# Score sums of batches 0 to 3 on TensorE by accumulating transposes, and two GpSimd product batches instead of three

## What is computed

```python
# s: attention over the HEADS of one token (16 x 16 scores for each token)
q = rope(xn @ Wq + bq);  k, v = split((xn @ Wdown + bdown) @ Wup + bup);  k = rope(k)
att = softmax(einsum('bthd,btgd->bthg', q, k) / sqrt(8))
s = einsum('bthg,btgd->bthd', att, v).reshape(B, T, 128) @ Wout + bout
# g: silu of a block over the other axis: attention along the batch axis, then a
# mixture of 8 experts (2 per token, 1280 rows of room each)
g = silu(h1 + moe_out)
```

## Time and profile before

| | us |
|---|---|
| median of 3 runs (404.27 to 406.10) | 405.15 |
| the profiled execution | 404.89 |
| its span, first to last instruction | 403.0 |
| VectorE busy | 367.4 |
| TensorE busy | 300.0 |
| GpSimd busy | 248.8 |
| ScalarE busy | 175.8 |

### The profile page before, as it was taken

One profiled execution on the slowest core, in us unless ns is written; L12 is line 12 of the kernel. 1 busy time (PEld: TensorE's weight loads), 2 busy tenths in 40 slices (PEclk: granted clock), 3 DMA queues, 4 the chain that ended last, 5 costly groups with the idle time before them and its releaser, 6 DMA issues.

```text
span 403.0 us, 5161 instructions
## 1 busy us (share of the span) xinstructions
PE 300.0 (74%) x1734; PEld 237.3 (59%) x1734; DVE 367.4 (91%) x499; ACT 175.8 (44%) x388; POOL 248.8 (62%) x268
## 2 busy tenths in 40 slices
PE   0846989495974473636267999999999999999890
PEld 0744567374663372236156679687779669668740
DVE  4999899979697999999999999999899999996666
ACT  2657383734172721110011667557672756561050
POOL 2397881892000577777773785587797777775271
PEclk9959899797896856959569899999999989999996
DMA  7599980000000111111113943213331321111936
GB/s 198 139 213 199 279 254 2 2 0 1 2 0 0 33 54 48 53 53 55 53 53 103 297 109 115 68 54 100 93 101 46 114 72 54 39 54 48 339 104 182
DMA packets 53719, 38.09 MB, mean 95 GB/s; under 512 B 5497, under 2 KB 50366, under 8 KB 53694
## 3 DMA queue, kind: packets, MB, share of 16 engines
q1 hardware_dynamic: 49086, 28.25, 28.0%
q0 software_dynamic: 4608, 9.51, 7.0%
HBM read 16.55 MB, written 21.20 MB: 94 GB/s over the span
## 4 chain that ended last, share of the span: by engine, by line
DVE 67%; PE 13%; issue 11%; ACT 5%; POOL 2%; DMA 2%; DVEq 0%; POOLq 0%; ACTq 0%
DVE prod L305 13%; DVE prod L297 12%; DVE score L651 12%; PE banks L831 4%; DVE stat L404 3%; DVE score L471 3%; POOL expert_rows L1420 2%; DVE score L638 2%; DVE hsum L675 2%; PE banks L992 2%; DVE hmax L669 2%; DVE prod L493 2%; PE banks L769 1%; DVE xn_all L526 1%; DVE flat L508 1%
## 5 line engine op out<-in xcount | busy, mean ns | idle before, releaser
L1392 POOL DMA_INDIRECT slot_rows<-rows_all,scatter_at x64 | 62.9, 982 | 60.5 <-DVE scatter_at L625 41.3
L1420 POOL DMA_INDIRECT expert_rows<-flat,to_at x80 | 79.8, 998 | 24.8 <-issue 20.9
L305 DVE TENSOR_TENSOR prod<-score,banks 128x2048 f32<-128x2048 f32 x32 | 70.9, 2268 | 3.5 <-PE banks L992 3.5
L992 PE MATMUL banks<-c_identf,prod 128*128 128x128 f32 x512 | 61.0, 282 | 13.2 <-DVE prod L305 13.2
L992 PEld LDWEIGHTS banks<-c_identf,prod 128*128 128x128 f32 x512 | 59.4, 147 | 14.3 <-DVE prod L305 14.3
L1355 POOL TENSOR_TENSOR prod<-rows_all,block_kv 128x64 f32<-128x64 f32 (+3 forms) x64 | 48.6, 794 | 16.1 <-ACT block_kv L1123 16.0
L297 DVE TENSOR_TENSOR prod<-banks,qkv_h 128x2048 f32<-128x2048 f32 x24 | 53.8, 2283 | 0.5
L651 DVE TENSOR_REDUCE score<-prod 128x512 f32<-128x4096 f32 x12 | 53.0, 4420 | 0.4
L962 PE MATMUL banks<-flat 128*128 128x512 f32 (+1 forms) x96 | 38.9, 550 | 4.4 <-ACT flat L1269 2.2
L856 PE MATMUL banks<-wx,qkv_h 128*128 128x128 f32 x192 | 31.8, 330 | 9.2 <-ACT qkv_h L1142 7.7
L831 PE MATMUL banks<-prod,c_identf 128*128 128x448 f32 (+7 forms) x128 | 37.8, 452 | 0.0
(11 more groups left out here) (196 smaller groups left out, 496.1 us busy)
## 6 DMA issues: line engine op xcount, KB each, us to landing
slot_rows<-prod SPq DMA_DIRECT2D x20, 264.0 KB, 7.9
flat<-slot_rows SPq DMA_DIRECT2D x16, 264.0 KB, 3.4
expert_rows<-prod SPq DMA_DIRECT2D x8, 512.0 KB, 6.0
flat<-expert_rows SPq DMA_DIRECT2D x8, 512.0 KB, 9.0
xn_all<-in_x SPq DMA_DIRECT2D x4, 512.0 KB, 4.8
flat<-in_w SPq DMA_DIRECT2D x16, 128.0 KB, 2.2
out<-rows_all SPq DMA_DIRECT2D x7, 256.0 KB, 3.2
expert_rows<-flat,to_at POOLq DMA_INDIRECT x80, 2.2
```

The lines of the kernel that those rows point to most:

```text
L305: return eng.tensor_tensor(value_pair(a // 2)[:, a % 2, :].rearrange("p (g h d) -> p g h d", g=H, h=H), p.rearrange("p h g -> p g h").unsq ...
L992: i = M.matmul(head_bank(s, p)[:, a * P:(a + 1) * P], value_pair(p)[:, a % 2, g * D:(g + 1) * D], C["identf"][:], is_transpose=True, start ...
L1392: Q.indirect_dma_start(slots_d, bass.IndirectOffsetOnAxis(ap=scatter_at[:, k, n:n + 1], axis=0), z2x[:, h, s, part], None, element_offset= ...
L1420: Q.indirect_dma_start(expert_d, bass.IndirectOffsetOnAxis(ap=to_at[:, e % 3, a:a + 1], axis=0), ye[:, e % 2, a, :], None).then_inc(ye_out ...
```

## The change

TensorE sums the score products of all pairs of batches 0 to 3. VectorE writes the products of such a pair with the channel outermost; TensorE transposes each 128 x 128 block with accumulation over the eight channels, which gives the sums turned (`turn_scores`); ScalarE copies them to SBUF (`keep_scores`); four transposes turn them back into PSUM (`turn_back`); VectorE takes maximum and difference from there. The reductions of these pairs are gone. GpSimd keeps batches 5 and 6; the second pair of batch 4 goes to VectorE. The order is rewritten on three engines: TensorE's projections of k now wait for `index_done` and stand between the new groups, and batch 2's `sum_values`, batch 1's `attention_out`, and the projections of v for batch 3 and q for batch 5 stand ahead of expert 0. Expert 0 additionally waits for `differences(3)`, since banks 0 and 1 hold scores until then.

```diff
-PE_SCORES, SCORE_BANK = 1, 0
-POOL_SCORES = {4: 0, 5: 1, 6: 3}
+PE_SCORES = (0, 1, 2, 3)
+POOL_SCORES = {5: 0, 6: 2}
...
-EXPONENTIAL_AFTER = {1: 3, 3: 4, 4: 5, 6: 6}
-COPY_AFTER = {0: 5, 2: 6}
-TURN_AT = {1: 2, 3: 3, 4: 4, 6: 5}
-OUT_AFTER = {0: 1, 2: 2, 4: 3, 5: 4, 7: 5}
-SUMS_AFTER = {1: 2, 3: 3, 4: 4, 6: 5}
-V_AFTER = {0: 3, 2: 4, 4: 5, 5: 6, 7: 7}
-Q_AFTER = {0: 5, 2: 6, 4: 7}
+EXPONENTIAL_AFTER = {1: 4, 3: 5, 4: 6, 6: 7}
+COPY_AFTER = {1: 6}
+TURN_AT = {1: 3, 3: 4, 5: 5}
+OUT_AFTER = {0: 2, 2: 3, 4: 4, 6: 5}
+SUMS_AFTER = {1: 3, 3: 4, 5: 5}
+V_AFTER = {0: 4, 2: 5, 4: 6, 6: 7}
+Q_AFTER = {1: 6, 2: 7}
...
-            return prodB if (s, p) <= (PE_SCORES, 0) else prodC
+            return pool_prod if s in PE_SCORES and p == 1 else prodC
...
+                if s in PE_SCORES:
+                    wait_past(dve, "scores_turned", 2 * (s - 1) + p + 1)
...
+            def turn_scores(s, p):
+
+                pe.wait_ge(W["q_read"], 2 * s + p + 1)
+                wait_past(pe, "row_diff", s)
+                for i in range(2):
+                    for c in range(2):
+                        at = slice((2 * i + c) * P, (2 * i + c + 1) * P)
+                        for d in range(HD):
+                            m = M.matmul(bank[p][:, at], score_pair(s, p)[:, i, (2 * d + c) * P:(2 * d + c + 1) * P], C["identf"][:],
+                                         is_transpose=True, start=(d == 0), stop=(d == HD - 1))
+                m.then_inc(W["scores_turned"], 1)
+
+            def turn_back(s, p):
+
+                pe.wait_ge(W["scores_kept"], 2 * s + p + 1)
+                for j in range(TT):
+                    i = M.transpose(bank[p][:, j * P:(j + 1) * P], turned_scores[:, p, j * P:(j + 1) * P], C["identf"][:])
                 i.then_inc(W["qk_summed"], 1)
...
+            pe.wait_ge(W["row_diff"], len(PE_SCORES))
             q_read(2)
             for e in range(E):
                 expert(e)
...
+            def keep_scores(s, p):
+                act.wait_ge(W["scores_turned"], 2 * s + p + 1)
+                A.copy(turned_scores[:, p], bank[p]).then_inc(W["scores_kept"], 1)
```

More of the change, by code:

```diff
@@ L655, in differences @@
             def differences(s):
-                if s == PE_SCORES:
+                if s in PE_SCORES:
                     half = TT * H // 2
-                    parts = [(rows(bank[SCORE_BANK]), slice(0, half)), (rows(score[:, s % 2, half * H:]), slice(half, 2 * half))]
-                    dve.wait_ge(W["qk_summed"], 1)
-                    for src, at in parts:
+                    parts = [(rows(bank[p]), slice(p * half, (p + 1) * half)) for p in range(2)]
+                    for p, (src, at) in enumerate(parts):
+                        dve.wait_ge(W["qk_summed"], 2 * s + p + 1)
                         i = V.tensor_reduce(hmax[:, s % 2, at], src, AX_X, ALU.max)
@@ L733, in _ @@
             pairs(0, 1)
+            pairs(1, 0)
+            differences(0)
+            pairs(1, 1)
             for s in range(S):
[L735 to L741, removed]
                 if s == S - 2:
-                    differences(s + 1)
+                    differences(S - 1)
                 totals(s)
@@ L748, in _ @@
                 values(s, 1)
+                if s + 1 < S - 1:
+                    differences(s + 1)
+                if s + 2 < S:
+                    pairs(s + 2, 0)
+                    pairs(s + 2, 1)
+                if s < S // 2 - 1:
+                    normalize(s)
             for p in range(2):
@@ L1038, in attention_out_last @@
                 i.then_inc(W["attn_ready"], 1)
+            pe.wait_ge(W["index_done"], 1)
+            project_k(1)
+            project_k(2)
+            turn_scores(0, 0)
+            project_k(3)
+            turn_scores(0, 1)
+            project_k(4)
+            turn_back(0, 0)
+            project_k(5)
+            turn_back(0, 1)
             project_v(1)
-            for s in range(1, S):
-                project_k(s)
+            project_k(6)
             project_q(2)
+            project_k(7)
+            turn_scores(1, 0)
             project_q(3)
-            pe.wait_ge(W["index_done"], 1)
+            turn_scores(1, 1)
             pe.wait_ge(W["k_kept"], S)
-            sum_scores()
             turn_sums(0)
+            turn_back(1, 0)
+            turn_back(1, 1)
             sum_values(0, 0)
             sum_values(0, 1)
+            turn_scores(2, 0)
+            turn_scores(2, 1)
             project_q(4)
+            turn_back(2, 0)
+            turn_back(2, 1)
             attention_out(0)
@@ L1057, in _ @@
             sum_values(1, 1)
+            turn_scores(3, 0)
+            turn_scores(3, 1)
+            project_q(5)
+            turn_back(3, 0)
+            turn_back(3, 1)
+            attention_out(1)
+            project_v(3)
+            turn_sums(2)
+            sum_values(2, 0)
+            sum_values(2, 1)
+            pe.wait_ge(W["row_diff"], len(PE_SCORES))
             q_read(2)
@@ L1308, in _ @@
             keep_k(1)
+            keep_k(2)
             rows_of_slots(2)
-            keep_k(2)
+            keep_scores(0, 0)
+            keep_k(3)
+            keep_scores(0, 1)
+            keep_k(4)
+            keep_k(5)
             rows_of_slots(3)
-            for s in range(3, S):
-                keep_k(s)
             exponentials(0)
+            keep_k(6)
+            keep_k(7)
+            keep_scores(1, 0)
+            keep_scores(1, 1)
             widen_share(0)
@@ L1322, in _ @@
             exponentials(2)
+            keep_scores(3, 0)
+            keep_scores(3, 1)
+            copy_q(5)
+            keep_attention(1)
+            widen_share(2)
+            keep_share(2)
+            exponentials(3)
             for e in range(E):
@@ L1330, in _ @@
                     copy_q(COPY_AFTER[e])
-            exponentials(7)
             for s in (S - 2, S - 1):
```

40 lines of the change are left out of this document (17 added, 23 removed).

## The result

The changed kernel takes 393.89 us in the median (390.71 to 396.68), beside 405.62 us for the kernel before: a ratio of 0.963, with a 95% interval of 0.953 to 0.973. The forecast was 394.0. The ratios leave out executions more than 1.5% above the fastest of the same kernel (the profiled one of the changed kernel is among these), so they are not the quotients of the medians.

A forecast was written before the change was run, and what follows sets the result against it. It took TensorE's expert stage as the bound: -11.43 moved work, -1.22 old waits, +0.8 and +0.7 new waits make -11.15 us, from 405.15 to 394.0 us. Forecast 390 to 398.5 (70%), wider range 390 to 403.

The forecast's parts named there:

- TensorE's stage bounds, not VectorE's sum: In the expert stage, TensorE's 139.1 us set the time; over half of VectorE's 26.5 us saving would not be seen.
- The rival with all 26.5 us in it (378.7): VectorE was the only bound, so its whole net saving of 26.5 us shows: 378.7 us; chance 4%.
- -11.43 us of moved work: Work leaving TensorE's expert stage: value sums of batch 2 6.99, output and two projections 3.84, turned sums 0.60 us.
- The waits: TensorE's two waits for VectorE go (-1.22 us); new ones come at `tail_start` (+0.8) and behind expert 0 for `normalize(2)` (+0.7).
- A term that I set to nothing: Clock at expert 0's products: a TensorE that comes warm gains up to 1.6 us, left outside the sum.
- Expert 0's start: VectorE waits 3.5 us, `values(2)` ends at 212.8, `sum_values(2)` at 219.8; expert 0 starts when its rows land, as before.
- The margin of 0.7 us: Between the end of `sum_values(2)` and expert 0's start: 0.7 us, with every further microsecond paid in full.
- Restarts of the clock: Rival: short TensorE waits in batches 0 and 1 drop the clock, four restarts cost 8 us, about 401 us; chance 15%.
- the lower level through the stage: Rival: TensorE's clock stays low through most work ahead of the experts, near 411 or up to 445 us; chance 7%.
- GpSimd sets nothing: GpSimd loses a product of 2 x 4.53 us and a wait of 8.2; its last scatters still follow expert 7.
- The tail unchanged: From `tail_start` to the end the code is the same and still takes 43 us.
- VectorE idle ahead of `values(7)`: Near the end VectorE stands idle 15 us or more in all, as `values(7)` needs the first half of `sum_values(6)`.

The follow-up runs named there:

- moves_back: Changed kernel with the five TensorE groups moved back behind expert 0, score sums still on TensorE: median 404.75 us, 1.003 of the kernel before.
- spare_later_exp: spare_stage with ScalarE's exponentials of batch 6 one expert later, behind expert 5: median 393.86 us, 257.6 us from the first score product.
- before_moves: Kernel before with only the five TensorE groups moved ahead of the experts, score sums left on VectorE: median 426.82 us, 1.046 of before.
- before_two: Kernel before with GpSimd making score products of batches 5 and 6 only, VectorE those of batch 4: median 407.94 us, 0.996 of before.
- six_first: Changed kernel with the turning and value sums of batch 6 ahead of the tail's start products: median 392.51 us, 255.9 us from the first score product.
- pool_three: Changed kernel with GpSimd making score products of batches 4, 5 and 6 as before: median 408.39 us, 272.0 us from the first score product.
- spare_early: Changed kernel with one unused 4.42 us VectorE reduction added behind batch 1's value products, ahead of the experts: median 400.68 us.
- spare_stage: Changed kernel with one unused 4.42 us VectorE reduction added behind batch 4's value products, in mid expert stage: median 395.01 us.
- after_again: Changed kernel measured a second time with no edit: median 392.77 us, 0.968 of the kernel before.

## Why the prediction held, step by step

- **TensorE's stage bounds, not VectorE's sum.** Right. VectorE lost 31.8 us of work, the kernel gained 12.4. moves_back shows it directly: with VectorE's relief and without the moves, nothing is gained. spare_later_exp shows it from the other side: 4.42 us more on VectorE cost nothing. The rival with all 26.5 us in it (378.7) is out.
- **-11.43 us of moved work.** Right: undoing the moves costs 12.8, and before_moves, with the moves alone, has a stage 11.6 us shorter than before.
- **The waits.** The two old ones (-1.22) are gone. The new ones were +0.8 and +0.7 in the sum and are 0.85 and 1.08. But that the old ones go because VectorE is relieved of the reductions is not shown. In before, one of VectorE's differences took 5.60 instead of 1.2 us beside GpSimd's products (297.08, see the end), and from there VectorE works without a break to both normalizings that TensorE waited for (322.08 and 355.98). With 4.4 us less there, by these rows, neither wait would have come, nor the fall of the clock behind the first (next point): up to 2.5 of the 13.05 us, as an estimate, may come from where GpSimd's products lie now. No run separates the two: before_two has no such meeting, but one pair of products, 4.48 us, more on VectorE.
- **A term that I set to nothing.** The stage became 13.05 us shorter, where my terms give 11.15. The measured waits and the moved work make -11.43 - 1.22 + 0.85 + 1.08 = -10.72. The rest is the clock. Expert 0 up to its last product took 220.54 to 233.16 before and 225.40 to 237.86 - 1.08 = 236.78 after, 1.24 us less (I had that as "up to 1.6" outside the sum). And before, the clock fell behind the wait of 0.78 at expert 5 as well. I had read the row at 322.82 for its wait and not the rows behind it. The kernel before:

```profile
324.86 1.84 PE L856 MATMUL banks<-wx,qkv_h 128*128 128x128 f32 x8
326.49 2.17 PE L955 MATMUL banks<-c_identf,flat 128*128 128x128 f32 x10
328.58 4.54 PE L962 MATMUL banks<-flat 128*128 128x512 f32 x12
```

  1.84 and 2.17 us stand where 1.06 and 1.25 are usual, 1.7 us, of which 0.36 replace the usual wait for ScalarE: 1.3 us. With it the sum is -13.3, against -13.05 measured. That 394.0 stands so near 393.89 is in part luck: the two stretches of lower clock (2.5 us) were not in the sum, the later start (0.7) went the other way, and whole times of this kernel spread by 6 us.
- **Expert 0's start.** VectorE's way was right to half a microsecond: waits of 3.7 us (3.5 forecast; 1.4 of them ahead of the third pair, which the working didn't have, as the first group took 4.97 us and held the products' buffer so long), `values(2)` ended 216.56 - 137.37 = 79.2 us after the first product (79.6 forecast). The margin of 0.7 us was not enough all the same, because `sum_values(2)` took 8.87 us (8.71 to the next start, where the sum has 6.99), at a clock of 0.72: expert 0 started 0.66 us later than before. Where it ran in 7.21 us (six_first), expert 0 waited for its rows again, 86.6 us after the first product.
- **Restarts of the clock, and the lower level through the stage.** Both out: the first group took 4.97 us (forecast near 4), the others 3.66 to 3.72, and the clock stood at 1.00 from 147 to 216 us, behind waits of 2.06 and 2.03 us too. One fall of the kind came, at 216, behind a wait of 1.57; it cost 1.7 us. In 147 to 180 us TensorE did little but transposes and small projections. The Trainium skill, "TensorE: Matmul & The Clock Gate", section "Part 4: PE-mode transpose", says that transposes don't count as activity in the same way; for these accumulating float32 transposes the traces of before (0.50 to 1.00 within one burst of them) and of after (1.00 from 147 to 180 us) both disagree.
- **GpSimd sets nothing.** Right for the change as made, but too short. I had costed only what GpSimd's lost product frees (nothing, before_two), not what it would hold up if it stayed (14.6 us, pool_three).
- **The tail unchanged, VectorE idle ahead of `values(7)`.** Right: 43.3 us and 17.9 us (15 or more forecast).

## What to carry to other kernels

When one engine is taken off a long chain, the gain is what the next engine can do with the earlier data: here nearly all of it came from work that could be moved out of TensorE's stage, and neither the relief nor the moves gained anything alone. Look for an engine's slack on every way by which it is waited for, also through a third engine's program order (exponentials ahead of an expert's copy). And read not only the wait but the rows behind it: a wait on TensorE can cost as much again in the clock (1.7 us of longer wait and 1.6 of clock in spare_early).

## What the runs showed of the hardware

- A wait of TensorE was often followed by a stretch at a lower granted clock, but not by its length alone: 0.78 us in before, 0.84 in moves_back, 0.96 in spare_later_exp, 2.75 in spare_early and 3.30 in spare_stage each lost a further 1.3 to 1.7 us, the 5.95 us in pool_three about 4; 1.08, 2.03 and 2.06 us in after lost nothing, and the 1.57 us ahead of `sum_values(2)` lost 1.7 us in after and nothing in six_first. What decides it I can't tell from these rows. The granted clock behind three of these waits, from pool_three, spare_early and spare_stage:

```profile
236.50:242.00 5.50, 5.29 (x17) 0.50 0.15 52
```

```profile
241.00:247.00 6.00, 5.73 (x28) 0.72 0.13 44
```

```profile
306.90:311.00 4.10, 4.05 (x7) 0.61 0.60 158
```

- The same code up to the first score product took from 130.87 us (six_first) to 137.85 us (after_again). The clock differs there too: between 20 and 60 us it was 0.70 in after and 0.87 in six_first. That spread is more than half of this change's gain, and why the traces are compared from a common moment.
- VectorE's difference of 128x1024 (subtraction, both inputs and the result in SBUF) met a product of GpSimd three times in the twelve traces, and was longer each time: 5.60 us in before (297.08), 2.59 in before_moves (321.95), 1.93 in pool_three (248.26). The other 54 took 1.22 to 1.33. The rows of before:

```profile
297.08 5.60 DVE L670 TENSOR_TENSOR score<-score,hmax 128x1024 f32<-128x1024 f32 x1
```

```profile
292.59 9.00 POOL L297 TENSOR_TENSOR qkv_h<-block_kv,qkv_h 128x2048 f32<-128x2048 f32 x2
```

  All three ended 1.08 or 1.09 us behind the end of the product that they met (301.59, 323.46 and 249.10), as if the difference began only then. The maxima just ahead of them (1.21 us each, as elsewhere) ran beside the same products. After has no such meeting, and 4.4 of the 5.3 us that VectorE lost beyond my sum are this. No run was made to test it.
